# Twelve layers on one core: every root as an exponential of half a logarithm, under one activation table set

## The reference

```python
def _layernorm(x, axis=-1, eps=1e-05):
    m = jnp.mean(x, axis=axis, keepdims=True)
    v = jnp.var(x, axis=axis, keepdims=True)
    return (x - m) / jnp.sqrt(v + eps)

x = x + _L0_xattn_ref(_layernorm(x, axis=-1), ctx_4096, ctx_4096, ...)
...
x = x + _L3_ffn_ref(_layernorm(x, axis=-1), L3_ffn_codebooks, ...)
```

## Time and profile before

| | |
|---|---|
| device time, three runs | 1756.38, 1752.21, 1755.44 us; median 1755.44 |
| profiled execution | span 1752.0 us from the first to the last instruction; what lies around the span is not listed for it |
| PE busy | 1581.9 us (90%) |
| DVE busy | 1074.7 us (61%) |
| ACT busy | 922.2 us (53%), 37 table loads of 1.283 us among it |
| L0x, L3x | about 505 and 539 us |

### The profile page before, as it was taken

The page is one execution under the profiler, slowest core; times in us unless marked ns, Lnnn a source line. Parts: engine busy times, 40 slices in busy tenths (PEclk is TensorE's granted clock), DMA queues, the critical chain, the costliest instruction groups (busy, mean ns, idle before and its releaser), DMA issues. The chain is left out here.

```text
span 1752.0 us, 23311 instructions
## 1 busy us (share of the span) xinstructions
PE 1581.9 (90%) x7553; PEld 1199.3 (68%) x7553; DVE 1074.7 (61%) x2216; ACT 922.2 (53%) x1592; POOL 283.8 (16%) x248
## 2 busy tenths in 40 slices
PE   4999999999989768797899978968999999999996
PEld 4788788878864333684666647847877877877863
DVE  5666666666667942574788836646476476476473
ACT  4554554555455411452388855536556556556552
POOL 0000000000003410342266634500000000000000
PEclk9999999999999879899999989979999999999997
DMA  7011010111064043451622115441100101101011
GB/s 260 15 40 57 24 60 36 33 51 38 22 240 161 0 165 99 156 166 72 153 30 32 21 70 159 137 180 37 37 24 36 60 24 37 58 24 42 18 55 76
DMA packets 32555, 131.65 MB, mean 75 GB/s; under 512 B 5184, under 2 KB 7360, under 8 KB 23792
## 3 DMA queue, kind: packets, MB, share of 16 engines
q1 hardware_dynamic: 32496, 130.94, 22.5%
HBM read 125.16 MB, written 0.26 MB: 72 GB/s over the span
## 5 line engine op out<-in xcount | busy, mean ns | idle before, releaser
L1878 POOL TENSOR_TENSOR L2x_p_lo<-L2x_e_t,L2x_p_hi 128x512 fp32r<-128x512 f32 x80 | 105.1, 1324 | 63.2 <-ACT L2x_p_hi L2063 62.5
L746 DVE TENSOR_TENSOR L0x_k_lo<-bank,L0x_k_hi 128x512 fp32r<-128x512 f32 x128 | 85.7, 688 | 42.5 <-ACT L0x_k_hi L635 42.0
L746 DVE TENSOR_TENSOR L3x_k_lo<-bank,L3x_k_hi 128x512 fp32r<-128x512 f32 x128 | 85.4, 688 | 40.0 <-ACT L3x_k_hi L635 39.9
L389 PE MATMUL bank<-L0x_ctx_hi,L0x_w_hi 128*128 128x512 f32 x256 | 103.7, 405 | 4.2 <-DVE L0x_ctx_lo L661 4.2
L389 PE MATMUL bank<-L3x_ctx_hi,L3x_w_hi 128*128 128x512 f32 x256 | 102.8, 401 | 4.2 <-DVE L3x_ctx_lo L661 4.2
L635 ACT ACTIVATE L0x_k_hi<-bank 128x512 fp32r<-128x512 f32 x128 | 74.2, 599 | 54.7 <-PE bank L511 54.7
L635 ACT ACTIVATE L3x_k_hi<-bank 128x512 fp32r<-128x512 f32 x128 | 73.9, 599 | 53.2 <-PE bank L511 53.2
L390 PE MATMUL bank<-L3x_ctx_lo,L3x_w_hi 128*128 128x512 f32 x256 | 101.2, 395 | 0.0
L391 PE MATMUL bank<-L3x_ctx_hi,L3x_w_lo 128*128 128x512 f32 x256 | 101.1, 395 | 0.0
L391 PE MATMUL bank<-L0x_ctx_hi,L0x_w_lo 128*128 128x512 f32 x256 | 101.0, 394 | 0.0
L390 PE MATMUL bank<-L0x_ctx_lo,L0x_w_hi 128*128 128x512 f32 x256 | 100.2, 391 | 0.0
(11 more groups left out here) (630 smaller groups left out, 4374.5 us busy)
## 6 DMA issues: line engine op xcount, KB each, us to landing
L0x_w_kqv<-in_L0x_kqv SPq DMA_DIRECT2D x7, 1536.0 KB, 6.3
L3x_w_kqv<-in_L3x_kqv SPq DMA_DIRECT2D x7, 1536.0 KB, 6.4
L0x_w_o<-in_L0x_o SPq DMA_DIRECT2D x8, 1024.0 KB, 4.9
L1a_w_o<-in_L1a_o SPq DMA_DIRECT2D x8, 1024.0 KB, 7.4
L2a_w_o<-in_L2a_o SPq DMA_DIRECT2D x8, 1024.0 KB, 7.4
L3x_w_o<-in_L3x_o SPq DMA_DIRECT2D x8, 1024.0 KB, 4.8
L0x_s<-in_ctx_t SPq DMA_DIRECT2D x4, 1024.0 KB, 12.7
L0a_w<-in_L0a_w SPq DMA_DIRECT2D x4, 1024.0 KB, 10.7
```

The lines of the kernel that those rows point to most:

```text
L389: pe.matmul(out, left[0], right[0], start=start, stop=False)
L746: dve.tensor_tensor(p_lo[:, kt % 4, :], ring_bank(kt)[:], bits(p_hi[:, kt % 4, :]), ALU.subtract).then_inc(p_ready, 1)
L1878: pool.tensor_tensor(p_lo[:, t % 8, :], e_of(t), bits(p_hi[:, t % 8, :]), ALU.subtract).then_inc(low_pool, 1)
```

## The change

Each root becomes two ACT instructions. Ln takes over scale and small bias that Sqrt had, writes the logarithm, an own semaphore is waited for, and Exp with scale -0.5 writes one over the root. The reciprocal on DVE goes, and in LayerNorm and L3f also the addition of 1e-5. In L2a Exp has the scale +0.5, which gives the root itself, and DVE's addition and reciprocal stay; both pieces share one Exp. ACT preloads the set `natural_log_exp_and_others` during `load_start`. The constant `zero` becomes `tiny` (1e-30).

```diff
@@ class LayerNorm, vector and scalar
         steps.then(dve.bn_stats(self.stats[:], core.x[:]))
-        steps.then(dve.bn_aggr(self.mean_var[:], self.stats[:]))
-        dve.tensor_scalar(veps, self.mean_var[:, 1:2], 1e-5, None, ALU.add).then_inc(self.var_ready, 1)
-        dve.wait_ge(self.std_ready, 1)
-        steps.then(dve.reciprocal(rstd, std))
-        dve.tensor_scalar(self.xn[:], core.x[:], self.mean_var[:, 0:1], rstd, ALU.subtract,
+        dve.bn_aggr(self.mean_var[:], self.stats[:]).then_inc(self.var_ready, 1)
+        dve.wait_ge(self.rstd_ready, 1)
+        dve.tensor_scalar(self.xn[:], core.x[:], self.mean_var[:, 0:1], self.small[:, 1:2], ALU.subtract,
                           ALU.mult).then_inc(self.xn_ready, 1)
...
         act.wait_ge(self.var_ready, 1)
-        act.activation(self.small[:, 1:2], self.small[:, 0:1], ACT.Sqrt).then_inc(self.std_ready, 1)
+        act.activation(self.small[:, 0:1], self.mean_var[:, 1:2], ACT.Ln,
+                       bias=self.core.eps5[:]).then_inc(self.log_ready, 1)
+        act.wait_ge(self.log_ready, 1)
+        act.activation(self.small[:, 1:2], self.small[:, 0:1], ACT.Exp, scale=-0.5).then_inc(self.rstd_ready, 1)
@@ class ContextKeys, scalar (scalar_context has the same for four tiles at once)
-            act.activation(self.rms_k[:, kt:kt + 1], self.sumsq_k[:, kt:kt + 1], ACT.Sqrt,
-                           bias=self.core.eps6[:], scale=1.0 / D).then_inc(self.rms_k_ready, 1)
+            act.activation(self.log_k[:, kt:kt + 1], self.sumsq_k[:, kt:kt + 1], ACT.Ln,
+                           bias=self.core.eps6[:], scale=1.0 / D).then_inc(self.log_k_ready, 1)
+            act.wait_ge(self.log_k_ready, kt + 1)
+            act.activation(self.rstd_k[:, kt:kt + 1], self.log_k[:, kt:kt + 1], ACT.Exp,
+                           scale=-0.5).then_inc(self.rstd_k_ready, 1)
@@ class ContextKeys, vector
             j = kt // 4
-            dve.wait_ge(self.rms_f_ready, j + 1)
-            dve.reciprocal(self.rstd_f[:, 4 * j:4 * j + 4], self.rms_f[:, 4 * j:4 * j + 4]).then_inc(self.rstd_f_ready, 1)
             dve.wait_ge(self.rstd_f_ready, j + 1)
...
-        if 1 <= kt <= KT:
-            dve.wait_ge(self.rms_k_ready, kt)
-            dve.reciprocal(self.rstd_k[:, kt - 1:kt], self.rms_k[:, kt - 1:kt]).then_inc(self.rstd_k_ready, 1)
@@ latent attention, scalar (L1x's query norm and L3f's dots change in the same way)
-                bias = core.eps5[:] if eps_inside else core.zero[:]
-                act.activation(rstd[:, 0:1], sumsq[:, 0:1], ACT.Sqrt, bias=bias, scale=1.0 / QR).then_inc(rms_ready, 1)
-                act.activation(rstd[:, 1:2], sumsq[:, 1:2], ACT.Sqrt, bias=bias, scale=1.0 / KR).then_inc(rms_ready, 1)
+                bias = core.eps5[:] if eps_inside else core.tiny[:]
+                act.activation(sumsq[:, 0:1], sumsq[:, 0:1], ACT.Ln, bias=bias, scale=1.0 / QR).then_inc(log_ready, 1)
+                act.activation(sumsq[:, 1:2], sumsq[:, 1:2], ACT.Ln, bias=bias, scale=1.0 / KR).then_inc(log_ready, 1)
+                act.wait_ge(log_ready, 2)
+                act.activation(rstd[:], sumsq[:], ACT.Exp, scale=-0.5 if eps_inside else 0.5).then_inc(rms_ready, 1)
@@ latent attention, vector
                 if not eps_inside:
                     steps.then(dve.tensor_scalar(rstd[:], rstd[:], 1e-6, None, ALU.add))
-                steps.then(dve.reciprocal(rstd[:], rstd[:]))
+                    steps.then(dve.reciprocal(rstd[:], rstd[:]))
@@ load_start
+            @block.scalar
+            def _(act):
+                act.preload_act_table_set("natural_log_exp_and_others")
```

More of the change, by code:

```diff
@@ L100, in __init__ @@
         self.eps6 = sb("eps6", [P, 1])
-        self.zero = sb("zero", [P, 1])
+        self.tiny = sb("tiny", [P, 1])
         self.bank = [ctx.enter_context(nc.psum_tensor(f"bank{i}", [P, 512], F32)) for i in range(8)]
@@ L167, in __init__ @@
         self.mean_var = st.sb("ln_mean_var", [P, 2])
-        self.small = st.sb("ln_small", [P, 3])
+        self.small = st.sb("ln_small", [P, 2])
         self.own = st.sem("ln_own")
         self.var_ready = st.sem("ln_var_ready")
-        self.std_ready = st.sem("ln_std_ready")
+        self.log_ready = st.sem("ln_log_ready")
+        self.rstd_ready = st.sem("ln_rstd_ready")
         self.xn_ready = st.sem("ln_xn_ready")
@@ L177, in vector @@
         core, steps = self.core, Steps(dve, self.own)
-        veps, std, rstd = (self.small[:, i:i + 1] for i in range(3))
         steps.then(dve.bn_stats(self.stats[:], core.x[:]))
-        steps.then(dve.bn_aggr(self.mean_var[:], self.stats[:]))
-        dve.tensor_scalar(veps, self.mean_var[:, 1:2], 1e-5, None, ALU.add).then_inc(self.var_ready, 1)
-        dve.wait_ge(self.std_ready, 1)
-        steps.then(dve.reciprocal(rstd, std))
-        dve.tensor_scalar(self.xn[:], core.x[:], self.mean_var[:, 0:1], rstd, ALU.subtract,
+        dve.bn_aggr(self.mean_var[:], self.stats[:]).then_inc(self.var_ready, 1)
+        dve.wait_ge(self.rstd_ready, 1)
+        dve.tensor_scalar(self.xn[:], core.x[:], self.mean_var[:, 0:1], self.small[:, 1:2], ALU.subtract,
                           ALU.mult).then_inc(self.xn_ready, 1)
@@ L786, in __init__ @@
         self.sumsq_f = work.sb("sumsq_f", [P, KT])
-        self.rms_f = work.sb("rms_f", [P, KT])
+        self.log_f = work.sb("log_f", [P, KT])
         self.sumsq_k = work.sb("sumsq_k", [P, KT])
-        self.rms_k = work.sb("rms_k", [P, KT])
+        self.log_k = work.sb("log_k", [P, KT])
         self.rstd_k = work.sb("rstd_k", [P, KT])
@@ L796, in __init__ @@
         self.squared_f = sem("squared_f")
-        self.rms_f_ready = sem("rms_f_ready")
+        self.log_f_ready = sem("log_f_ready")
         self.rstd_f_ready = sem("rstd_f_ready")
@@ L801, in __init__ @@
         self.squared_k = sem("squared_k")
-        self.rms_k_ready = sem("rms_k_ready")
+        self.log_k_ready = sem("log_k_ready")
         self.rstd_k_ready = sem("rstd_k_ready")
@@ L855, in scalar_context @@
         act.wait_ge(self.squared_f, 4 * j + 4)
-        act.activation(self.rms_f[:, 4 * j:4 * j + 4], self.sumsq_f[:, 4 * j:4 * j + 4], ACT.Sqrt,
-                       bias=self.core.eps6[:], scale=1.0 / D).then_inc(self.rms_f_ready, 1)
+        act.activation(self.log_f[:, 4 * j:4 * j + 4], self.sumsq_f[:, 4 * j:4 * j + 4], ACT.Ln,
+                       bias=self.core.eps6[:], scale=1.0 / D).then_inc(self.log_f_ready, 1)
+        act.wait_ge(self.log_f_ready, j + 1)
+        act.activation(self.rstd_f[:, 4 * j:4 * j + 4], self.log_f[:, 4 * j:4 * j + 4], ACT.Exp,
+                       scale=-0.5).then_inc(self.rstd_f_ready, 1)
     def scalar(self, act, kt):
@@ L1511, in codebook_ffn @@
         var_ready = st.sem("var_ready")
-        std_ready = st.sem("std_ready")
+        log_ready = st.sem("log_ready")
+        rstd_ready = st.sem("rstd_ready")
         top_ready = st.sem("top_ready")
@@ L1563, in _ @@
                 act.wait_ge(var_ready, 1)
-                act.activation(scal[:, 1:2], scal[:, 0:1], ACT.Sqrt).then_inc(std_ready, 1)
+                act.activation(scal[:, 1:2], mean_var[:, 1:2], ACT.Ln, bias=core.eps5[:]).then_inc(log_ready, 1)
+                act.wait_ge(log_ready, 1)
+                act.activation(scal[:, 2:3], scal[:, 1:2], ACT.Exp, scale=-0.5).then_inc(rstd_ready, 1)
                 act.wait_ge(top_ready, 1)
@@ L1578, in _ @@
                 steps.then(dve.bn_stats(stats[:], core.bank[4][:, 0:N]))
[L1579 to L1582, removed]
+                dve.bn_aggr(mean_var[:], stats[:]).then_inc(var_ready, 1)
+                dve.wait_ge(rstd_ready, 1)
                 steps.then(dve.tensor_scalar(dots[:], core.bank[4][:, 0:N], mean_var[:, 0:1], scal[:, 2:3],
@@ L1647, in feature_cross_attention @@
         q_squared = st.sem("q_squared")
+        log_q = st.sem("log_q")
         rms_q = st.sem("rms_q")
@@ L1705, in _ @@
                 act.wait_ge(q_squared, 1)
-                act.activation(rstd_q[:], sumsq_q[:], ACT.Sqrt, bias=core.eps6[:], scale=1.0 / D).then_inc(rms_q, 1)
+                act.activation(sumsq_q[:], sumsq_q[:], ACT.Ln, bias=core.eps6[:], scale=1.0 / D).then_inc(log_q, 1)
+                act.wait_ge(log_q, 1)
+                act.activation(rstd_q[:], sumsq_q[:], ACT.Exp, scale=-0.5).then_inc(rms_q, 1)
                 act.wait_ge(max_ready, 1)
@@ L1728, in _ @@
                 dve.wait_ge(rms_q, 1)
-                steps.then(dve.reciprocal(rstd_q[:], rstd_q[:]))
                 dve.scalar_tensor_tensor(q_sb[:], q_sb[:], rstd_q[:], row_sb[:, 2, :], ALU.mult,
@@ L2667, in _ @@
                 pool.memset(core.ones_r[:].bitcast(F32), 1.0)
-                pool.memset(core.zero[:], 0.0)
+                pool.memset(core.tiny[:], 1e-30)
                 pool.memset(core.eps5[:], 1e-5)
                 pool.memset(core.eps6[:], 1e-6)
+            @block.scalar
+            def _(act):
+                act.preload_act_table_set("natural_log_exp_and_others")
 def store_result(core, out):
```

2 lines of the change are left out of this document (1 added, 1 removed).

## The result

The changed kernel takes 1740.95 us, the median of 5 runs (1738.53 to 1744.71), where the kernel before takes 1755.44 in the same comparison. The ratio is 0.9923, with a 95% interval of 0.9901 to 0.9944: 13.5 us faster, 10 to 17. A second comparison gave 1738.69 us and a ratio of 0.9910 (0.9888 to 0.9932). The prediction was 1740.8, 14.6 us faster.

The account below looks back on a forecast made before the run. In L3x, DVE's chain behind the exponential, delayed by table loads, was taken to hold up PE. L3x 11.8 + layer norms 1.6 + L0a 1.5 - others 0.3 = 14.6 us, giving 1740.8 us; own range 1737 to 1744, whole range 1735 to 1748.

Parts of the forecast that it names:

- L3x, the exponential's load: In each L3x group, without the load ahead of the exponential, it and DVE's whole chain start 1.28 us earlier.
- The catch-up behind the first score: In L3x, DVE reaches the first score 1.3 us earlier, then takes 0.61 instead of 0.69 us per score until reaching PE.
- The fall-back of 1.36: In L3x, a group gains 1.36 us instead of 1.50 if its end moves by DVE's first 1.3 alone.
- rival (a): In L3x, PE wins only its shown wait, 8.2 us, 11.0 in all, 1744.4 us; chance 0.15.
- L3x, the logarithm's load: In L3x, PE's gap ahead of the second sum of squares goes, and all that follows from PE moves by 0.22 us.
- Layer norms: Statistics to scaling takes 0.56 us, 0.18 less with a load and 0.06 less without; 1.6 us in all.
- L0a: DVE's reciprocals go, 0.07 us per key tile and 0.21 per context, 1.7 us; the last tile adds 0.2; net 1.5.
- The 0.3 us for L1x, L1a and L2a: An added Exp of 0.23 us, with L2a keeping its reciprocal, costs these stages 0.03, 0.03 and 0.23 us.
- (b): Rival: the table loads stay and split roots add more, 13.1 us slower, 1768.5 us; chance 0.03.
- (c): Rival: all loads across the kernel are paid in full, 37 x 1.28 = 47 us gained, 1708 us; chance 0.01.
- (d): Rival: Exp from the shared set is slower per column, in the wide groups' softmax; at 3.0 us, 1775 us; chance 0.01.
- (e): Rival: denser PE work gets a lower clock; 1% of L3x gives back 5 us, 1746 us; chance 0.05.

Follow-up runs that it names:

- Ln's load back: Changed kernel with one table load put back ahead of the first logarithm in each of L3x's eight groups; 1746.2 us, ratio 0.9952 to the kernel before.
- Exp by chunk: Changed kernel with L3x's exponential in five parts, each behind its logarithm, and DVE's product made chunk by chunk; 1741.86 us, ratio 0.9926 to the kernel before.
- the set for L3x alone: Kernel before, old roots kept, with one preload of the shared set behind L3x's layer norm; 1747.59 us, ratio 0.9952 to the kernel before.
- roots alone: Changed kernel with both table loads put back in each group of L3x, the new roots kept; 1754.65 us, ratio 0.9992 to the kernel before.
- Exp's load back: Changed kernel with one table load put back ahead of the exponential in each group of L3x; 1752.68 us, ratio 0.9985 to the kernel before.

## Why the prediction was right

**L3x, the exponential's load: right.** 1.28 us a group was forecast, by a start 1.28 earlier and a DVE chain that moves with it; put back by itself it costs 1.29. That DVE would then be last by 0.3 us was shown by the exponential in five parts, which takes most of DVE's work behind the last exponential away and lets the first score start 0.28 earlier. The catch-up behind the first score, which I called tight, holds: from the exponential's start to the first score, the first transposes and the next group's first sum of squares, a steady group has the same distances before and after, to 0.04 us (9.73, 24.18 and 48.65 against 9.73, 24.17 and 48.61 us in one group of each). The fall-back of 1.36 and rival (a) are out.

**L3x, the logarithm's load: right in place, too small.** 0.22 was forecast; the change is worth 65.35 - 63.70 - 1.29 = 0.36, and by itself the load costs 0.34. The gap itself is the 0.22 to 0.23 that I read. The step I had wrong is that all that follows moves by the gap alone: the stretch behind it is longer too, 3.35 us in the trace of before (1253.77 to 1257.12), 3.30 in its repeat and 3.29 with the load put back, instead of 3.20, at a granted clock of 1.00 in all. I hadn't compared that stretch with an undisturbed one. About 0.08 of it stands between the first two matmuls behind the gap; why they are further apart stays open.

**L3x in sum: 11.8 forecast, 11.5 in the stage,** 11.0 between the repeated traces, and that it lies so near is luck, two errors that cancel. Steady groups gain 1.65 instead of 1.50, but the first gains only 0.44 (65.12 to 64.68), with its clock down from 1.00 to 0.97. Had it gained what the others did, the stage would have given 12.7.

**Layer norms: right.** 0.57 for 0.56, with Ln at 0.29 and Exp at 0.20 as taken; 8 x 0.17 + 3 x 0.05 = 1.5 us for 1.6.

**L0a: right in mechanism, too large.** From the first to the last tile's context product, the single lines of before and after:

```profile
L898 DVE SCALAR_TENSOR_TENSOR L1kw_raw<-bank,L1k_rstd_f,L1kw_row x16: 739/741/753, 543.4 to 621.0; 128x512 f32<-128x512 f32 x16
```

```profile
L903 DVE SCALAR_TENSOR_TENSOR L1kw_raw<-bank,L1k_rstd_f,L1kw_row x16: 739/742/752, 543.6 to 619.9; 128x512 f32<-128x512 f32 x16
```

By the starts in the timelines 77.5 us became 76.3. It is 76.3 or 76.4 in all seven traces with the new roots, and 77.5, 77.5 and 78.7 in the three with the old. A tile lost 0.06 to 0.07 (4.23 to 4.17), one with a context reciprocal 0.27 (4.44 to 4.17), as read from the earlier trace rows. But one tile grew by 0.22 (5.58 to 5.80): in it DVE starts a product while one of POOL's runs, and now 0.3 us earlier in it; that product took 2.84 us instead of 2.55, in before and after:

```profile
584.45 2.85 POOL L1010 TENSOR_TENSOR L0a_prod_pool<-L0a_qkv,L0a_s 128x1024 f32<-128x1024 f32 x1 [10.94 <-DVE L0a_prod L1086]
586.41 2.55 DVE L1086 TENSOR_TENSOR L0a_prod<-L0a_qkv,L0a_s 128x1024 f32<-128x1024 f32 x1
```

```profile
583.96 2.84 POOL L1012 TENSOR_TENSOR L0a_prod_pool<-L0a_qkv,L0a_s 128x1024 f32<-128x1024 f32 x1 [10.87 <-DVE L0a_prod L1088]
585.64 2.84 DVE L1088 TENSOR_TENSOR L0a_prod<-L0a_qkv,L0a_s 128x1024 f32<-128x1024 f32 x1
```

So DVE's part is 1.2 us instead of 1.7, and with the forecast's 0.2 for the tail, which no run isolates, 1.0 net instead of 1.5.

**Outside L3x in all** 2.8 us was forecast (14.6 - 11.8). Span less L3x is 1213.9, 1219.6 and 1213.3 us in the three traces with the old roots, and from 1209.1 to 1214.8, on average 1211.9, in the seven with the new: 3.7 less on average, with 6 us between traces of one kind. It fits the sum and can't test it closer. The 0.3 us for L1x, L1a and L2a remains argued only.

**The rivals.** (b) and (c): one load is left, and the other 36 gave 14 us, not 47. (d): the softmax exponentials take 2008 ns on 2048 columns, as with the old set. (e): the steady groups have a clock of 1.00 at 63.29 us of work in 63.67, so denser work is granted no less there.

Only the first group is lower, in seven of the eight traces of edited kernels and in neither of before. The traces show where. In the first group PE pauses ahead of its first three transposes of the weights and again behind them, 0.97 and 1.77 us, in all but one trace (there it is 1.13 and 1.77). In three traces the clock stays at the upper level through it, in seven it goes down to the lower one (1.2 GHz) during the second pause or just behind it. It stays there for 3.4 us in four of them (after, its repeat, Ln's load back, Exp by chunk) and for 6.8 us in three (the set for L3x alone, roots alone, Exp's load back). The transposes behind the second pause and a window from there, before and after, then a window of the roots alone (columns of the earlier trace rows):

```profile
1226.16 1.64 PE L511 MATMUL bank<-ident,L3x_s 128*128 128x128 f32 x13 [1.77 <-ACT L3x_s L629]
1226.00:1232.00 6.00, 5.74 (x37) 4.87 (x38) 3.95 (x7) 3.74 (x9) 0.03 (x1) 1.00 0.00 0
```

```profile
1227.71 2.50 PE L512 MATMUL bank<-ident,L3x_s 128*128 128x128 f32 x13 [1.77 <-ACT L3x_s L630]
1228.00:1232.00 4.00, 4.00 (x21) 3.61 (x20) 2.67 (x4) 2.28 (x4) 0.00 (x0) 0.57 0.00 0
```

```profile
1222.80:1229.60 6.80, 6.09 (x23) 5.46 (x24) 3.03 (x5) 3.64 (x7) 0.00 (x0) 0.50 0.00 0
```

From the first of these transposes to the next projections it is 21.0 us without the lower level, 22.2 to 22.3 with 3.4 us of it and 23.4 to 23.5 with 6.8: it costs 1.2 and 2.5 us. Without it the changed kernel's first group would have gained 0.44 + 1.2 = 1.7 us, as the steady ones did. The loads don't decide it: the kernel with two loads ahead of the exponential keeps the upper level, the one with one load has 6.8 us of the lower. Nor does denser work, since the roots alone, with groups as before, have 6.8 us too. Why the clock goes down in one trace and not in another behind the same pauses stays open.

The profiled span, 1741.4, lies 4 us above the 1737.4 forecast: against before L0f is 2.3 longer and L1x 1.1, the first group's lower clock costs 1.2, and L3a is 2.2 shorter. The repeat came to 1736.7. That the median met the forecast of 1740.8 within 0.2 us is luck as well: the repeat's median is 2.3 us lower, and the interval of the gain is 7 us wide.

## What to carry to other kernels

Read what stands in front of each function on ACT, not only the functions: a logarithm and an exponential that take turns in a loop can reload a table every time, and one preload of a set that holds both took L3x's 16 loads away without a line of the arithmetic changed. What a load costs is decided where its result is needed: 1.29 us a group ahead of an exponential that DVE and PE wait for, 0.34 ahead of a logarithm that only frees a bank, about 0.1 ahead of a layer norm's root (0.74 against 0.62 us), nothing for the softmax loads outside L3x, as far as spans that differ by 6 us among themselves can tell. Where the times vary by several us, compare one repeated group in the traces; at an equal clock it told 0.1 us apart here.

## What the runs showed of the hardware

- A load of the set that is already active is carried out and takes the same 1283 ns (the exponential's load put back, 8 of them).
- DVE's product of 1024 elements in L0a takes 1.88 us, and 2.55 or 2.84 when it starts 1.96 or 1.68 us after one of POOL's of 2.85 us has begun and so runs beside it (kernel before and changed kernel).
- The granted clock of short stages differs between executions of one program: L0f 0.65 and 0.86, 14.8 and 12.5 us. These are shares of a stretch at the two levels of 1.2 and 2.4 GHz, and in L0f alone they are worth more than the layer norms gained in all (2.3 against 1.5 us).
- Behind the same two pauses of PE (0.97 and 1.77 us in L3x's first group) the clock stayed at 2.4 GHz in three traces and went down to 1.2 GHz in seven, for 3.4 or 6.8 us, which cost 1.2 or 2.5 us.
- Behind a break of 0.23 us in PE's stream the second matmul follows the first after 0.31 us instead of 0.23, at a clock that the trace gives as 1.00 (the logarithm's load put back).
